# Attention in a stack of layers on one core: a head's 36 key blocks exponentiated in nine chunks of four instead of twelve chunks by tile

## The chip, the cores and the metric

One core of one Trainium2 chip runs the whole program. The metric is the device time of one execution in microseconds. It has five engines with queues of their own: TensorE (PE, matmuls), VectorE (DVE), ScalarE (ACT), GpSimd (POOL) and SyncE (SP, which issues DMAs).

## The reference, cut to what matters

The program computes a stack of layers on 1024 tokens of 512 features: a feed-forward layer, a Mamba2 layer, feed-forward layers again, attention, and a last feed-forward layer. The change touches the attention's heads alone. For each of 32 heads of 16 features (8 key/value heads):

```
draft = einsum(q, k) + causal
_, draft_indices = top_k(draft, 128)
mask = neg except 0 at draft_indices; neg above the diagonal
scores = einsum(q, k) / sqrt(16) + mask
attn = softmax(scores)
out = attn @ v
```

So each row of the 1024 x 1024 causal triangle keeps its 128 largest scores, and the softmax runs over these.

## The kernel before, in words

A head's triangle is cut into 8 tiles of 128 query rows; tile t has t + 1 key blocks of 128, 36 blocks in all. The function `attention_heads_fast` (from line 1824) runs rounds n, and in one round four heads are at different stages. Each engine has its own program, written out by hand; an engine waits on semaphores in the order of its program and nothing overtakes.

- Head n + 1: PE makes its scores into `ps_z` (`scores`, L1933), and DVE copies them to `z` and takes the row maxima (`evacuate`, L2216). Tile 0 is first, with a small `sample` (L1922); these begin the round.
- Heads n, n - 1: ACT counts how many scores lie above a trial cut, four sweeps of seven ACTIVATEs each in a round (`count`, L2052); POOL moves the cuts after each sweep (`move`, L2132) and hands over the final cut (L2171) after the fourth.
- Head n - 2: for tiles 1 to 7 DVE marks what is above the cut (`take`, L2229), PE makes the scores again with the marks (`marked_scores`, L1949) into `ps_m`, DVE finds the eight largest that are left and replaces them (`pick`, L2247: MAX8 at L2256, MATCH_REPLACE8 at L2264), writing `picked`. `marked_scores` of a tile waits for the `pick` before it, and `pick` waits for `marked_scores`. Tile by tile DVE runs `pick(t)`, `evacuate(t)`, `take(t + 2)`.
- Head n - 3: PE makes the exponents transposed into one of two PSUM tiles `ps_e` (`exponents`, L1982), ACT exponentiates them into one of three slots of `eT` (`exponential`, L2067, the ACTIVATE at L2074), and PE multiplies by v (`add_v`, L2007, the matmul at L2016; 32-bit, 17 columns, two matmul instructions a block). After the last chunk DVE divides (`divide`, L2267) in the next round.
- The row maxima of head n - 2 are turned by PE (`turned_rows`, L1970) and copied by ACT to `rows` in two halves (`row_out`, L2077). The second half ends ACT's round, and it waits until the last chunk's exponents of head n - 3 are made.

A head's exponents come in chunks. Before, a chunk is up to four blocks of one tile, so there are 12: of 1, 2, 3, 4 blocks for tiles 0 to 3, and 4 + 1, 4 + 2, 4 + 3, 4 + 4 for tiles 4 to 7. For each chunk PE issues one matmul a block from `picked` (L1995, not for tile 0), one wide matmul with the row maxima (L1997), one a block for the scores (L2000) and one for the diagonal block (L2003). `turn_and_add` (L2020) makes the exponents of a chunk and then `add_v` of the chunk two before. PE's round, from L2028:

```
if live(n - 3): turn_and_add(n - 3, CHUNK_AHEAD)          # chunk 0
if live(n + 1): scores(n + 1, 0); sample(n + 1)
if live(n - 3): turn_and_add(n - 3, CHUNKS_FIRST)         # chunk 1
for t in range(1, NT):
    marked_scores(n - 2, t)
    turn_and_add(n - 3, CHUNKS_AFTER_MARKED[t])
    scores(n + 1, t)
    if t in (2, 7): turned_rows(n - 2, t // 7)
    turn_and_add(n - 3, CHUNKS_AFTER_SCORES[t])
```

On ACT `EXP_BEFORE` (L1845) spreads the exponentials evenly over the 28 counts of a round, by the columns counted; each round does them one chunk late (`LATER`).

Of the kernel before, what the change touches and what calls it, by code (L numbers as in the profile page):

```python
# [15 lines left out]
ACT = mybir.ActivationFunctionType  # L16
AX = mybir.AxisListType

P = 128
S = 1024  # L20
D = 512
NT = S // P
# [24 lines left out]
REP = AH // KVH  # L47
# [1776 lines left out]
def attention_heads_fast(nc, env, X, qT, kT, v, mixed, q_tok, k_sums):  # L1824

    W = NT - 1
    OFF = [P * (t * (t + 1) // 2 - 1) for t in range(NT + 1)]
    FAR = 2.0 ** 20
    BIG = 1024.0
    RING = 3  # L1830
    CHUNKS = [(t, b) for t in range(NT) for b in range(0, t + 1, 4)]
    NCH = len(CHUNKS)
    LAST_CHUNK = [max(i for i, (u, _) in enumerate(CHUNKS) if u == t) for t in range(NT)]
    CHUNK_AHEAD = (0,)
    CHUNKS_FIRST = (1,)
    CHUNKS_AFTER_MARKED = ((), (), (), (), (), (7,), (9,), ())
    CHUNKS_AFTER_SCORES = ((), (2,), (3, 4), (5,), (6,), (8,), (10,), (11,))
    LATER = 1
    SWEEPS = ((0, 0), (1, 2), (0, 1), (1, 3))
    FIRST, LAST = -1, AH + 3  # L1840
# [6 lines left out]
    with ExitStack() as ctx:  # L1847
# [8 lines left out]
        picked = env.picked  # L1856
# [63 lines left out]
        @block.tensor  # L1920
        def _(pe):
            def sample(h):  # L1922

                if h >= 4:
                    pe.wait_ge(rows_done, 2 * (h - 3))
                if h >= 1:
                    pe.wait_ge(stats_done, 3 * h)
                for t in range(1, NT):
                    last = pe.matmul(ps_sample[:, t - 1, :], qT[:, h, t * P:(t + 1) * P], k_sums[:, h // REP, t, :],
                                     start=t == 1, stop=True, skip_group_check=True)  # L1930
                last.then_inc(sampled, 1)

            def scores(h, t):  # L1933

                L, at = (t + 1) * P, z_at(t)
                done = h * NT + t - (0 < t < 4)
                if done:
                    pe.wait_ge(z_done, done)
                for n in range(0, L, BANK):
                    w = min(BANK, L - n)  # L1940
                    diagonal = n + w == L
                    if diagonal:
                        pe.matmul(ps_z[:, at + L - P:at + L], env.ident_bf[:], env.future_bf[:], start=True, stop=False,
                                  skip_group_check=True)
                    last = pe.matmul(ps_z[:, at + n:at + n + w], qT[:, h, t * P:(t + 1) * P], kT[:, h // REP, n:n + w],  # L1945
                                     start=not diagonal, stop=True, skip_group_check=True)
                last.then_inc(s_done, 1)

            def marked_scores(h, t):  # L1949

                L, at = (t + 1) * P, m_at(t)
                pe.wait_ge(take_done, h * W + t)
                done = h * W + t - 1 - (1 < t < 4)
                if done:
                    pe.wait_ge(pick_done, done)
                for n in range(0, L, BANK):
                    w = min(BANK, L - n)
                    diagonal = n + w == L
                    if diagonal:
                        pe.matmul(ps_m[:, at + L - P:at + L], env.ident_bf[:], env.future_bf[:], start=True, stop=False,  # L1960
                                  skip_group_check=True)
                    pe.matmul(ps_m[:, at + n:at + n + w], qT[:, h, t * P:(t + 1) * P], kT[:, h // REP, n:n + w],  # L1962
                              start=not diagonal, stop=False, skip_group_check=True)
                for n in range(0, L, BANK):
                    w = min(BANK, L - n)
                    last = pe.matmul(ps_m[:, at + n:at + n + w], ident_taken[:], mark[:, (h * W + t) % 2, n:n + w], start=False, stop=True,  # L1966
                                     skip_group_check=True)
                last.then_inc(marked, 1)

            def turned_rows(h, half):  # L1970

                pe.wait_ge(split_done, h + 1)
                if half == 0 and h + 3 < AH:
                    pe.wait_ge(stats_done, 3 * (h + 4))
                elif half or h:
                    pe.wait_ge(rows_done, 2 * h + half)
                for t in range(4):
                    last = pe.matmul(ps_x[:, t * P:(t + 1) * P], parts[:, 4 * half + t, :], env.ident_bf[:],
                                     start=t == 0, stop=True, skip_group_check=True)
                last.then_inc(row_done, 1)  # L1980

            def exponents(h, i):  # L1982

                t, b0 = CHUNKS[i]
                w = min(4, t + 1 - b0)
                g = h * NCH + i
                if g >= 2:
                    pe.wait_ge(exp_done, g - 1)
                pe.wait_ge(rows_done, 2 * h + 1 + t // 4)
                out = ps_e[g % 2]  # L1990
                if t:
                    pe.wait_ge(pick_done, h * W + t)
                    for b in range(w):
                        at = OFF[t] + (b0 + b) * P
                        pe.matmul(out[:, b, :], picked[:, h % 2, at:at + P], ident_back[:], start=b == 0, stop=False,  # L1995
                                  skip_group_check=True)
                pe.matmul(out[:, 0:w, :], minus_rows[:], rows[:, t * P:(t + 1) * P].unsqueeze(1).to_broadcast([P, w, P]),  # L1997
                          start=t == 0, stop=False, skip_group_check=True)
                for b in range(w):
                    last = pe.matmul(out[:, b, :], kT[:, h // REP, (b0 + b) * P:(b0 + b + 1) * P], qT[:, h, t * P:(t + 1) * P],  # L2000
                                     start=False, stop=True, skip_group_check=True)
                if b0 + w == t + 1:
                    last = pe.matmul(out[:, w - 1, :], env.future_bf[:], env.ident_bf[:], start=False, stop=True,  # L2003
                                     skip_group_check=True)
                last.then_inc(et_done, 1)

            def add_v(g):  # L2007

                h, i = divmod(g, NCH)
                t, b0 = CHUNKS[i]  # L2010
                w = min(4, t + 1 - b0)
                pe.wait_ge(exp_done, g + 1)
                if i == 0 and h:
                    pe.wait_ge(divided, h)
                for b in range(w):
                    last = pe.matmul(ps_o[:, t, :], eT[:, g % 3, b * P:(b + 1) * P], v[:, b0 + b, h // REP, :],  # L2016
                                     start=i == 0 and b == 0, stop=b0 + b == t, skip_group_check=True)
                last.then_inc(av_done, 1)

            def turn_and_add(h, chunks):  # L2020

                for i in chunks:
                    exponents(h, i)
                    if h * NCH + i >= 2:
                        add_v(h * NCH + i - 2)

            pe.wait_ge(set_up, SET_UP)
            for n in range(FIRST, LAST):  # L2028
                if live(n - 3):
                    turn_and_add(n - 3, CHUNK_AHEAD)  # L2030
                if live(n + 1):
                    scores(n + 1, 0)
                    sample(n + 1)
                if live(n - 3):
                    turn_and_add(n - 3, CHUNKS_FIRST)
                for t in range(1, NT):
                    if live(n - 2):
                        marked_scores(n - 2, t)
                    if live(n - 3):
                        turn_and_add(n - 3, CHUNKS_AFTER_MARKED[t])  # L2040
                    if live(n + 1):
                        scores(n + 1, t)
                    if live(n - 2) and t in (2, 7):
                        turned_rows(n - 2, t // 7)
                    if live(n - 3):
                        turn_and_add(n - 3, CHUNKS_AFTER_SCORES[t])
            add_v(AH * NCH - 2)
            add_v(AH * NCH - 1)

        @block.scalar  # L2050
        def _(act):
# [14 lines left out]

            def exponential(g):  # L2067

                t, b0 = CHUNKS[g % NCH]
                w = min(4, t + 1 - b0)  # L2070
                act.wait_ge(et_done, g + 1)
                if g >= 3:
                    act.wait_ge(av_done, g - 2)
                act.activation(eT[:, g % 3, 0:w * P], ps_e[g % 2][:, 0:w, :].rearrange("p b q -> p (b q)"), ACT.Exp,  # L2074
                               scale=0.25).then_inc(exp_done, 1)

            def row_out(h, half):  # L2077
# [6 lines left out]
            for n in range(FIRST, LAST):  # L2084
                at = 0
# [364 lines left out]
```

## Time and profile before

| | |
|---|---|
| median of 3 runs | 3192.2 us (3191.99 to 3193.25) |
| the profiled execution, its own time | 3191.56 us |
| its span | 3189.8 us |
| mean granted TensorE clock | 0.949 of full |
| busy over the whole span | PE 90%, DVE 73%, ACT 62%, POOL 48% |
| the heads' rounds | from 2058.8 us (first row maximum of tile 0) to about 3064 us |
| ACTIVATEs at L2074, whole run | 384 (12 a head) |
| matmul instructions at L2016, whole run | 2304 (72 a head) |

The span is divided by engine busy time, and a share is an average over the whole program; the heads take the last third. Times in a row are from the span's start.

### The profile page before, as it was taken

What the parts mean: (1) busy time and instruction counts of PE and PEld (TensorE: products, weight loads), DVE (VectorE), ACT (ScalarE), POOL (GpSimd) and SP (SyncE); (2) the same over time, 40 slices, a digit from 0 to 9 for tenths busy, and PEclk for the clock granted to TensorE, in tenths of its full rate; (3) what the DMA queues carried; (4) which work ended last, traced back from release to release, by engine and by line L of the source; (5) the groups of instructions that cost most, each with busy time, mean ns of one, the idle gap of its engine ahead of it and who ended that gap; (6) DMA issues with size and microseconds to landing.
All of it is one profiled execution on the core that took longest, in us unless ns stands there. A gap on an engine that the chain in (4) does not pass through costs nothing. (4 is left out here: it accounts for less than half of the span.)

```text
span 3189.8 us, 50575 instructions
## 1 busy us (share of the span) xinstructions
PE 2886.2 (90%) x15929; PEld 1745.3 (55%) x15929; DVE 2319.5 (73%) x4516; ACT 1984.2 (62%) x4218; POOL 1539.0 (48%) x3659
## 2 busy tenths in 40 slices
PE   8899999999999999999999989748888888888779
PEld 4455455454464554554554544426666666666654
DVE  6666676676776766766766767758888888888746
ACT  2464554564554645545645623589999999999823
POOL 3235234253253352342442544677777777777503
PEclk9999999999999999999999999859988988988889
DMA  2222232132132231322322410000000000000010
GB/s 95 60 83 90 73 104 75 66 119 86 64 109 80 80 99 66 98 81 73 110 63 73 118 37 27 1 1 2 2 2 2 2 2 2 2 2 2 1 51 27
DMA packets 65804, 169.63 MB, mean 53 GB/s; under 512 B 11776, under 2 KB 19328, under 8 KB 64512
## 3 DMA queue, kind: packets, MB, share of 16 engines
q1 hardware_dynamic: 54448, 115.17, 11.3%
q10 hardware_dynamic: 11088, 51.19, 4.6%
q8 instruction: 132, 2.16, 0.3%
q14 instruction: 136, 1.11, 0.1%
HBM read 161.08 MB, written 5.24 MB: 52 GB/s over the span
## 5 line engine op out<-in xcount | busy, mean ns | idle before, releaser
L2063 ACT ACTIVATE X<-ah_z,ah_trial 128x256 bf16<-128x256 f32 (+6 forms) x896 | 732.9, 824 | 23.9 <-POOL ah_trial L2166 14.3
L1212 ACT ACTIVATE m_mix<-m_mix,m_cs 128x128 f32<-128x128 f32 x1024 | 312.5, 388 | 33.0 <-DMA m_mix<-cs_rows 32.7
L2016 PE MATMUL ah_ps_o<-a_v,X 128*128 128x17 f32 x2304 | 318.9, 265 | 0.2 <-DVE hT L2274 0.2
L2016 PEld LDWEIGHTS ah_ps_o<-a_v,X 128*128 128x128 f32 x2304 | 303.4, 200 | 0.3 <-issue 0.3
L1094 POOL TENSOR_TENSOR m_xdec<-m_xdt,m_decay_out 128x512 f32<-128x512 f32 x112 | 118.4, 1057 | 336.2 <-DVE m_xdt L1338 202.4
L1224 ACT ACTIVATE m_squares<-m_gate 128x512 f32<-128x512 f32 x128 | 80.5, 629 | 316.4 <-DVE m_gate L1376 316.2
L2256 DVE MAX8 ah_top<-ah_ps_m 128x8 f32<-128x256 f32 (+6 forms) x224 | 186.2, 831 | 73.2 <-PE ah_ps_m L1966 68.7
L1016 PE MATMUL m_ps_d<-m_w_out,m_gate 128*128 128x512 f32 x512 | 233.5, 599 | 0.0
L1016 PE MATMUL m_ps_x<-m_w_out,m_gate 128*128 128x512 f32 x512 | 233.0, 598 | 0.0
L2074 ACT ACTIVATE X<-ah_ps_e 128x512 f32<-128x512 f32 (+3 forms) x384 | 184.9, 482 | 53.7 <-PE ah_ps_e L2003 44.8
L1122 POOL TENSOR_TENSOR m_squares<-m_squares 128x256 f32<-128x256 f32 x128 | 92.9, 726 | 255.0 <-ACT m_squares L1224 255.0
L2235 DVE TENSOR_SCALAR_CACHE_REDUCE X<-ah_z,ah_cut 128x256 bf16<-128x256 f32 (+6 forms) x224 | 193.5, 874 | 26.2 <-POOL ah_cut L2171 26.2
L1962 PE MATMUL ah_ps_m<-a_kT,a_qT 128*128 128x512 bf16 (+3 forms) x352 | 117.2, 372 | 97.2 <-DVE tables L2264 97.2
L1338 DVE TENSOR_TENSOR m_xdt<-m_ps_y,m_dt 128x512 f32<-128x512 f32 x128 | 87.6, 690 | 160.4 <-PE m_ps_y L957 160.4
L2158 POOL TENSOR_TENSOR ah_slope<-ah_between,ah_table 128x7 f32<-128x7 f32 x128 | 193.3, 1511 | 0.0
L2226 DVE TENSOR_SCALAR_CACHE_REDUCE ah_z<-ah_ps_z 128x256 f32<-128x256 f32 (+6 forms) x224 | 182.5, 816 | 13.9 <-PE ah_ps_z L1945 13.9
L2264 DVE MATCH_REPLACE8 tables<-ah_top,ah_ps_m 128x256 bf16<-128x256 f32 (+6 forms) x224 | 182.5, 815 | 0.3 <-issue 0.3
L1345 DVE TENSOR_TENSOR m_mix<-m_mix,m_cb 128x1024 f32<-128x1024 f32 x128 | 176.8, 1381 | 4.6 <-ACT m_mix L1215 4.4
L2063 ACT ACTIVATION_READ_ACCUMULATOR X<-ah_z,ah_trial 128x1 f32 x896 | 176.9, 197 | 0.0
L1185 ACT ACTIVATE m_xbc<-m_xbc 128x1024 f32<-128x1024 f32 x80 | 84.6, 1057 | 148.4 <-DVE m_xbc L1321 148.2
L1079 POOL TENSOR_TENSOR m_xdt<-m_w_proj 128x256 f32<-128x256 f32 x32 | 23.8, 742 | 287.1 <-PE m_ps_d L885 287.1
L1321 DVE SCALAR_TENSOR_TENSOR m_xbc<-m_b_tok,m_conv_p,m_xbc 128x1023 f32<-128x1023 f32 (+2 forms) x96 | 129.7, 1351 | 44.6 <-ACT m_xbc L1177 42.4
(318 smaller groups left out, 7470.9 us busy)
## 6 DMA issues: line engine op xcount, KB each, us to landing
m_mix<-cs_rows SPq DMA_DIRECT2D x128, 512.0 KB, 4.0
m_w_proj<-in_w_proj ACTq DMA_DIRECT2D x69, 512.0 KB, 3.3
m_fade<-fade_rows SPq DMA_DIRECT2D x224, 128.0 KB, 3.9
m_w_out<-in_w_out ACTq DMA_DIRECT2D x7, 2048.0 KB, 7.8
X<-in_x SPq DMA_DIRECT2D x8, 256.0 KB, 5.9
m_w_out<-in_w_out SPq DMA_DIRECT2D x1, 2048.0 KB, 9.9
x_away<-X SPq DMA_DIRECT2D x1, 2048.0 KB, 7.3
X<-x_away SPq DMA_DIRECT2D x8, 256.0 KB, 6.1
```

The costliest lines, as they stand in the source:

```text
L1016: last = pe.matmul(ps_out[c % 2], gate[:, half * 4 + i, c * P:(c + 1) * P], w_out[:, half * 4 + i, :], start=(half == 0 and i == 0), stop= ...
L1212: act.activation(mix[:, u % 3, h, :], mix[:, u % 3, h, :], ACT.Relu, bias=cs[:, c, h0 + h:h0 + h + 1], scale=-1.0).then_inc(lag_done, 1)
L1321: op = dve.scalar_tensor_tensor(out=acc, in0=src[:, 0:S - n], scalar=conv_p[:, g, j, TAPS - 1 - n:TAPS - n], in1=acc, op0=ALU.mult, op1=AL ...
L1345: dve.tensor_tensor(mix[:, u % 3], mix[:, u % 3], cb[:, c, :].unsqueeze(1).to_broadcast([P, HU, P]), ALU.mult).then_inc(mix_done, 1)
L2016: last = pe.matmul(ps_o[:, t, :], eT[:, g % 3, b * P:(b + 1) * P], v[:, b0 + b, h // REP, :], start=i == 0 and b == 0, stop=b0 + b == t, s ...
L2063: act.activation(sign[:, at % 2, 0:(t + 1) * P], z[:, h % RING, cols(t)], ACT.Sign, bias=trial[:, h % RING, 0, t - 1:t], scale=-1.0, accum ...
L2074: act.activation(eT[:, g % 3, 0:w * P], ps_e[g % 2][:, 0:w, :].rearrange("p b q -> p (b q)"), ACT.Exp, scale=0.25).then_inc(exp_done, 1)
L2158: pool.tensor_tensor(slope[:, 0], between[:, 1], table[:, 5], ALU.pow).then_inc(own, 1)
L2226: dve.tensor_scalar(z[:, h % RING, cols(t)], ps_z[:, z_at(t):z_at(t) + (t + 1) * P], 0.0, NEG, ALU.add, ALU.max, accum_out=row_max[:, h % ...
L2235: dve.tensor_scalar(mark[:, (h * W + t) % 2, 0:(t + 1) * P], z[:, h % RING, cols(t)], cut[:, h % 2, t - 1:t], 0.0, ALU.is_ge, ALU.add, acc ...
L2256: dve.max(top[:, r], ps_m[:, m_at(t):m_at(t) + (t + 1) * P]).then_inc(pick_step, 1)
L2264: dve.match_replace(picked[:, h % 2, cols(t)], top[:, r], ps_m[:, m_at(t):m_at(t) + (t + 1) * P], TAKEN).then_inc(pick_done, 1)
```

## The change

It cuts the 36 blocks, in order of tile and block, into nine chunks of four. A chunk may then hold blocks of up to three tiles: (0,0) (1,0) (1,1) (2,0) | (2,1) (2,2) (3,0) (3,1) | (3,2) (3,3) (4,0) (4,1) | (4,2) (4,3) (4,4) (5,0) | (5,1) to (5,4) | (5,5) (6,0) (6,1) (6,2) | (6,3) to (6,6) | (7,0) to (7,3) | (7,4) to (7,7). For each tile in a chunk the matmul with the row maxima is issued apart, so there are 15 of them a head instead of 12. On PE, chunk 0 and 1 keep their places, and chunks 2 to 8 are issued one after each `scores(t)`, t from 1 to 7. ACT's nine exponentials are spread by the same formula. The first waits of a chunk are for the last tile in it.

```diff
-    CHUNKS = [(t, b) for t in range(NT) for b in range(0, t + 1, 4)]
+    BLOCKS = [(t, b) for t in range(NT) for b in range(t + 1)]
+    CHUNKS = [BLOCKS[i:i + 4] for i in range(0, len(BLOCKS), 4)]
     NCH = len(CHUNKS)
-    LAST_CHUNK = [max(i for i, (u, _) in enumerate(CHUNKS) if u == t) for t in range(NT)]
+    LAST_CHUNK = [max(i for i, blocks in enumerate(CHUNKS) if (t, t) in blocks) for t in range(NT)]
     CHUNK_AHEAD = (0,)
     CHUNKS_FIRST = (1,)
-    CHUNKS_AFTER_MARKED = ((), (), (), (), (), (7,), (9,), ())
-    CHUNKS_AFTER_SCORES = ((), (2,), (3, 4), (5,), (6,), (8,), (10,), (11,))
+    CHUNKS_AFTER_SCORES = ((), (2,), (3,), (4,), (5,), (6,), (7,), (8,))
...
             def exponents(h, i):
-                t, b0 = CHUNKS[i]
-                w = min(4, t + 1 - b0)
                 g = h * NCH + i
                 if g >= 2:
                     pe.wait_ge(exp_done, g - 1)
-                pe.wait_ge(rows_done, 2 * h + 1 + t // 4)
+                pe.wait_ge(rows_done, 2 * h + 1 + CHUNKS[i][-1][0] // 4)
+                pe.wait_ge(pick_done, h * W + CHUNKS[i][-1][0])
                 out = ps_e[g % 2]
...
+                tiles = sorted(dict(CHUNKS[i]))
+                for t in tiles:
+                    places = [n for n, block in enumerate(CHUNKS[i]) if block[0] == t]
+                    lo, w = places[0], len(places)
...
+                    pe.matmul(out[:, lo:lo + w, :], minus_rows[:], rows[:, t * P:(t + 1) * P].unsqueeze(1).to_broadcast([P, w, P]),
+                              start=first, stop=False, skip_group_check=True)
...
             def add_v(g):
...
-                for b in range(w):
-                    last = pe.matmul(ps_o[:, t, :], eT[:, g % 3, b * P:(b + 1) * P], v[:, b0 + b, h // REP, :],
-                                     start=i == 0 and b == 0, stop=b0 + b == t, skip_group_check=True)
+                for n, (t, b) in enumerate(CHUNKS[i]):
+                    last = pe.matmul(ps_o[:, t, :], eT[:, g % 3, n * P:(n + 1) * P], v[:, b, h // REP, :],
+                                     start=i == 0 and n == 0, stop=b == t, skip_group_check=True)
...
-                    if live(n - 3):
-                        turn_and_add(n - 3, CHUNKS_AFTER_MARKED[t])
...
-                act.activation(eT[:, g % 3, 0:w * P], ps_e[g % 2][:, 0:w, :].rearrange("p b q -> p (b q)"), ACT.Exp,
+                act.activation(eT[:, g % 3], ps_e[g % 2][:].rearrange("p b q -> p (b q)"), ACT.Exp,
                                scale=0.25).then_inc(exp_done, 1)
```

## Rows read from the trace of the kernel before

**Rows 1.** Busy time by window: PE, PEld, DVE, ACT, POOL, granted clock, DMA, GB/s:
```profile
2170.50:2941.00 770.50, 640.90 (x5908) 518.48 (x5906) 673.74 (x1795) 741.22 (x1822) 571.21 (x2055) 0.90 0.01 2
...
2377.80:2406.50 28.70, 23.74 (x234) 19.27 (x231) 25.95 (x70) 28.08 (x70) 22.02 (x80) 0.94 0.01 2
2406.50:2436.70 30.20, 24.91 (x233) 20.15 (x230) 25.93 (x70) 28.83 (x73) 21.96 (x80) 0.89 0.01 2
2436.70:2466.50 29.80, 24.85 (x230) 20.07 (x227) 25.82 (x69) 28.39 (x71) 21.88 (x80) 0.89 0.01 2
...
2438.00:2444.80 6.80, 5.78 (x38) 4.57 (x37) 6.18 (x24) 6.14 (x17) 5.95 (x25) 0.50 0.02 4
```
**Rows 2.** Line L2222, one instruction a round: count, first and last start:
```profile
L2222 DVE TENSOR_REDUCE ah_row_max<-ah_ps_z x27: 291/291/292, 2170.5 to 2941.0; 128x1 f32<-128x128 f32 x27
```
**Rows 3.** Waits, 2170.5 to 2941.0: who waited for whom, us, times, longest:
```profile
PE ah_ps_m L1962 <- DVE tables L2264: 75.2, 102, 1.2
DVE ah_top L2256 <- PE ah_ps_m L1966: 53.3, 78, 2.1
...
ACT X L2074 <- PE ah_ps_e L2003: 18.8, 41, 1.0
DVE ah_inv L2272 <- PE ah_ps_o L2016: 17.8, 26, 1.2
...
ACT ah_rows L2082 <- PE ah_ps_e L2003: 9.9, 26, 0.6
```
**Rows 4.** Timeline of ACT: start, us, engine, line, operation, shapes:
```profile
2434.70 0.58 ACT L2074 ACTIVATE X<-ah_ps_e 128x512 f32<-128x512 f32 x1
2435.18 0.61 ACT L2063 ACTIVATE X<-ah_z,ah_trial 128x384 bf16<-128x384 f32 x1
...
2437.30 0.26 ACT L2074 ACTIVATE X<-ah_ps_e 128x128 f32<-128x128 f32 x1
2437.45 0.93 ACT L2063 ACTIVATE X<-ah_z,ah_trial 128x768 bf16<-128x768 f32 x1
```
**Rows 5.** Timeline of DVE in a long round:
```profile
2438.08 0.21 DVE L2272 RECIPROCAL ah_inv<-ah_ps_o 128x8 f32<-128x8 f32 x1 [0.57 <-PE ah_ps_o L2016]
...
2438.53 0.47 DVE L2235 TENSOR_SCALAR_CACHE_REDUCE X<-ah_z,ah_cut 128x256 bf16<-128x256 f32 x1
...
2447.03 0.70 DVE L2256 MAX8 ah_top<-ah_ps_m 128x8 f32<-128x512 f32 x1 [1.90 <-PE ah_ps_m L1966]
```
**Rows 6.** Timeline of POOL at the same place:
```profile
2438.19 0.21 POOL L2171 TENSOR_TENSOR ah_cut<-ah_trial,ah_slope 128x7 f32<-128x7 f32 x1
```
**Rows 7.** Timeline of PE in that long round:
```profile
2436.33 0.23 PE L1943 MATMUL ah_ps_z<-future_bf,ident_bf 128*128 128x128 bf16 x1 [1.05 <-DVE ah_z L2226]
...
2436.64 0.27 PE L1995 MATMUL ah_ps_e<-ah_ident_back,tables 128*128 128x128 bf16 x2
...
2437.02 1.02 PE L2016 MATMUL ah_ps_o<-a_v,X 128*128 128x17 f32 x8
2439.06 0.29 PE L1960 MATMUL ah_ps_m<-future_bf,ident_bf 128*128 128x128 bf16 x1 [1.02 <-DVE X L2235]
...
2440.96 0.55 PE L2016 MATMUL ah_ps_o<-a_v,X 128*128 128x17 f32 x2
2441.35 0.27 PE L1960 MATMUL ah_ps_m<-future_bf,ident_bf 128*128 128x128 bf16 x1
...
2446.28 0.22 PE L1960 MATMUL ah_ps_m<-future_bf,ident_bf 128*128 128x128 bf16 x1
```
**Rows 8.** Timeline of PE in a short round, chunk 4 and its add_v:
```profile
2384.88 0.38 PE L1995 MATMUL ah_ps_e<-ah_ident_back,tables 128*128 128x128 bf16 x4
...
2385.54 0.79 PE L2016 MATMUL ah_ps_o<-a_v,X 128*128 128x17 f32 x6
2386.18 0.22 PE L1960 MATMUL ah_ps_m<-future_bf,ident_bf 128*128 128x128 bf16 x1
```
**Rows 9.** Timeline of DVE in that short round:
```profile
2386.94 0.70 DVE L2256 MAX8 ah_top<-ah_ps_m 128x8 f32<-128x512 f32 x1 [0.64 <-PE ah_ps_m L1966]
```

More of the change, by code:

```diff
@@ L1988, in exponents @@
                     pe.wait_ge(exp_done, g - 1)
-                pe.wait_ge(rows_done, 2 * h + 1 + t // 4)
+                pe.wait_ge(rows_done, 2 * h + 1 + CHUNKS[i][-1][0] // 4)
+                pe.wait_ge(pick_done, h * W + CHUNKS[i][-1][0])
                 out = ps_e[g % 2]
-                if t:
-                    pe.wait_ge(pick_done, h * W + t)
-                    for b in range(w):
-                        at = OFF[t] + (b0 + b) * P
-                        pe.matmul(out[:, b, :], picked[:, h % 2, at:at + P], ident_back[:], start=b == 0, stop=False,
-                                  skip_group_check=True)
@@ L1997, in exponents @@
-                pe.matmul(out[:, 0:w, :], minus_rows[:], rows[:, t * P:(t + 1) * P].unsqueeze(1).to_broadcast([P, w, P]),
-                          start=t == 0, stop=False, skip_group_check=True)
-                for b in range(w):
[L2000 to L2004, printed above, removed]
+                tiles = sorted(dict(CHUNKS[i]))
@@ new lines, in exponents @@
+                first = True
+                for t in tiles:
+                    places = [n for n, block in enumerate(CHUNKS[i]) if block[0] == t]
+                    lo, w = places[0], len(places)
+                    b0 = CHUNKS[i][lo][1]
+                    if t:
+                        for b in range(w):
+                            at = OFF[t] + (b0 + b) * P
+                            pe.matmul(out[:, lo + b, :], picked[:, h % 2, at:at + P], ident_back[:], start=first, stop=False,
+                                      skip_group_check=True)
+                            first = False
+                    pe.matmul(out[:, lo:lo + w, :], minus_rows[:], rows[:, t * P:(t + 1) * P].unsqueeze(1).to_broadcast([P, w, P]),
+                              start=first, stop=False, skip_group_check=True)
+                    first = False
+                    for b in range(w):
+                        last = pe.matmul(out[:, lo + b, :], kT[:, h // REP, (b0 + b) * P:(b0 + b + 1) * P],
+                                         qT[:, h, t * P:(t + 1) * P], start=False, stop=True, skip_group_check=True)
+                    if b0 + w == t + 1:
+                        last = pe.matmul(out[:, lo + w - 1, :], env.future_bf[:], env.ident_bf[:], start=False, stop=True,
+                                         skip_group_check=True)
@@ L2009, in add_v @@
                 h, i = divmod(g, NCH)
-                t, b0 = CHUNKS[i]
-                w = min(4, t + 1 - b0)
                 pe.wait_ge(exp_done, g + 1)
@@ L2014, in add_v @@
                     pe.wait_ge(divided, h)
-                for b in range(w):
-                    last = pe.matmul(ps_o[:, t, :], eT[:, g % 3, b * P:(b + 1) * P], v[:, b0 + b, h // REP, :],
-                                     start=i == 0 and b == 0, stop=b0 + b == t, skip_group_check=True)
+                for n, (t, b) in enumerate(CHUNKS[i]):
+                    last = pe.matmul(ps_o[:, t, :], eT[:, g % 3, n * P:(n + 1) * P], v[:, b, h // REP, :],
+                                     start=i == 0 and n == 0, stop=b == t, skip_group_check=True)
                 last.then_inc(av_done, 1)
@@ L2067, in exponential @@
             def exponential(g):
-                t, b0 = CHUNKS[g % NCH]
-                w = min(4, t + 1 - b0)
                 act.wait_ge(et_done, g + 1)
```

## The prediction

> **What bounds the kernel now.** The busy shares of the whole span put PE first, but they mix layers with different limits. What counts is the window view of 26 rounds of heads [rows 1, 2]: 770.5 us / 26 = 29.63 us a round, with ACT busy for 741.2 us of it (96%), DVE for 673.7 (87%), PE for 640.9 (83%). So ACT looks like the bound, with 741.22 / 26 = 28.51 us of work a round, and the change takes instructions from ACT. The Trainium skill (Perfetto Trace Analysis, Identifying the Most-Contended Engine) says to optimize the engine of highest occupancy first; by that, ACT is the place.
>
> The waits say otherwise [rows 3]. ACT's listed waits are all for PE: 18.8 us before an exponential, 9.9 before the row copy that ends its round, 1.1 us a round together. I find no listed wait of DVE or PE for ACT or POOL in these rounds. They wait for each other: PE 75.2 us for DVE's replaced maxima, DVE 53.3 us for PE's marked scores and 17.8 us for PE's last add_v before the division. Two engines that wait only for each other set their own length, and ACT follows with 1.1 us to spare. DVE is the longer half, 673.7 / 26 = 25.9 us of work a round, and its waits for PE are what can be won or lost.
>
> Where do these lie? In a long round 1.90 us is before the MAX8 of tile 3, and 0.57 before the division [rows 5]; in a short round the first is 0.64 [rows 9]. The windows show why [rows 1]. The long rounds (30.2 and 29.8 us, mean 30.0) have a mean granted clock of 0.89, the short one (28.7) 0.94. The low level, 1.2 of 2.4 GHz, lasts 6.8 us in a long round (the window at 0.50) and 2 x 0.06 x 28.7 = 3.4 us in the short one. Such a low spell follows two idle times of PE of 1.05 and 1.02 us [rows 7], and it covers the stretch in which PE has most to do before DVE can go on. With x the share of short rounds, 28.7 x + 30.0 (1 - x) = 29.63 makes x 0.28.
>
> **The change, part by part**, at full clock unless said.
>
> *ACT.* From start to next start an exponential of four blocks takes 0.48 us and one of one block 0.15 [rows 4]: 0.11 a block and 0.04 an instruction. Three instructions fewer save 3 x 0.04 = 0.12 us a round (ends: 0, and 3 x 0.15 = 0.45), some 4 us in 32 heads. ACT isn't on the path, so I count 0. Its idle time before exponentials should also go, since PE now makes chunks ahead of their places; what ACT wins it gives back at the row copy, which still waits for PE's last chunk.
>
> *PE's ring.* Exponents of chunk i wait for the exponential of chunk i - 2. By the kernel's formula exponential i starts (i + 1.3) x 28.4 / 9 us into ACT's round, which began at about 2434.2, 0.5 us before its first exponential [rows 4]: exponential 2 at 2444.6, over at 2445.2. PE reaches chunk 4 about 0.66 us after 2446.28 [rows 7], and perhaps 1.2 us earlier without a stall there, 2445.7. Tight, but later tiles have 75.2 / 102 = 0.7 us of idle time before each marked scores [rows 3], which covers a miss: 0, at worst 0.3 a round. The new wait of chunk 2 is for the second half of the row copy, over at 2434.2, and chunk 2 comes after 2439.06 [rows 7], 5 us later: 0. No DMA is issued or moved, and the queues of SP and POOL aren't touched.
>
> *The opening.* A chunk of four blocks of one tile takes 0.66 us and 3 blocks of add_v take 0.64, so 0.21 a block [rows 8]. Chunk 0 grows from one block to four of three tiles (+0.55, the two further row matmuls and diagonals in it), and the add_v before it from three blocks to four (+0.21). These 0.76 us stand in front of scores(0), where PE idles 1.05 us [rows 7]: 0, with 0.29 us of cover left. Chunk 1 grows from two blocks (0.38 us, 2436.64 to 2437.02, [rows 7]) to four with a diagonal (0.66 + 0.05): +0.33 us ahead of the add_v for which the division waits. DVE waits there already, and its next work is the first take of the round. POOL's cut is written from 2438.19 to 2438.40 and the take starts at 2438.53 [rows 5, 6], so nothing else held it. All of the 0.33 is on the path; at the low clock 0.67.
>
> *From the first to the third marked scores* PE works without a pause, 2439.06 to 2446.28 = 7.22 us [rows 7]. Chunk 2 gets one block more (+0.17), its add_v goes from 1 block to 4 (+0.64), that of chunk 1 from 2 to 4 (+0.43); old chunk 4 (0.66) and an add_v of 3 blocks (0.64) leave the stretch: -0.06 us. At the low clock a chunk's matmuls take double, and a block of add_v 0.39 (2440.96 to 2441.35, [rows 7]): 0.33 + 5 x 0.39 - 1.32 - 1.17 = -0.2. I take -0.1 (ends: -0.6, and +0.4 where the cover on DVE's side runs out at tile 2 first).
>
> *The later tiles.* After scores(3) PE has three blocks of a chunk more (+0.5), and 0.7 us of idle time for them; after tiles 5 and 6 it has less than before. 0; without that cover +0.5.
>
> *The clock.* Two things pull apart here, and no row shows which wins. PE's first idle time shrinks from 1.05 to 0.3 us, which speaks for fewer low spells. But the second stays at 1.02 or more, and the low stretch now carries eight blocks of 17-column add_v (four after chunk 2, four after chunk 3) where three stood (1 + 2). In the short round the clock rose again when PE had run chunk 2 with a single such block; that form doesn't come any more. The Trainium skill (TensorE: Matmul & The Clock Gate, What's actually happening) has the low level as the default, which activity lifts; no price follows from that here. I expect the spell in every round and the short form gone: 30.0 - 29.63 = +0.37 a round. In half the rounds I let it last another 3.4 us. Such an addition cost 30.0 - 28.7 = 1.3 us where nothing covered it; here it falls on tiles 3 and 4, with idle time beside it, and I take 0.8, so 0.4 a round. Ends: -1.2 (no spells, ACT binds) and +2.
>
> *Sum.* 0.33 - 0.1 + 0.37 + 0.4 = +1.0 us a round. 28 rounds have all four stages (n from 3 to 30), the three after them a part of it: I count 29, so +29 us. The profiled execution took 3191.56 us (its span 3189.8), 0.6 below the median: **3221 us**, 0.9% slower.
>
> **The rivals.**
>
> *The clock holds, and ACT binds: faster.* Place: the start of a round, between scores(0) and the first marked scores. If the filled idle time keeps the clock at its upper level, DVE's stalls at tiles 2 and 3 vanish. DVE's round is then 28.7 - 0.64 + 0.33 = 28.4 us and ACT's 28.51 - 0.12 = 28.4; both give -1.2 us a round, 29 x 1.2 = 35, so 3156 us. It decides from the point at which most rounds lose their low spell. For it: the idle times of 0.7 us before later marked scores are not followed by low spells in these rounds. Against: the 1 us before the first marked scores doesn't shrink. The occupancy rule above leads to the same place by another way, work taken from ACT. Chance 0.25.
>
> *The spells stay as they are.* 0.33 - 0.1 = +0.23 a round, 3198 us. For it: the two effects on the clock cancel. Chance 0.16.
>
> *The low clock feeds itself.* If PE at the low level, with four blocks of add_v to each chunk, becomes the longer half through tiles 3 to 5 too, the last term is 2 instead of 0.4: +2.6 a round, 3267 us. Against: it needs PE's later idle time gone in all rounds. Chance 0.12.
>
> The forecast has 0.47.
>
> **How the numbers follow.** About 0.2% (6.4 us) is what a measurement of this kernel can tell from no change. Faster by more than that: the first rival, 0.25. Within it: most of the second rival and a little of the forecast's low side, 0.13. Slower: the rest, 0.62. The forecast's own range is 3200 to 3240. To hold 8 in 10 the range goes some way toward both outer rivals: 3165 to 3250 leaves out over half of the first and most of the last.
>
> **What would show it.** Right: ACT's idle time before L2074 nearly gone, and that before L2082 at 1.5 us a round or more; the wait before L2272 up by 0.3; the MAX8 of 384 columns waiting over 1 us; a granted clock of 0.88 or lower over the rounds, and rounds of 30.6 us. Wrong: a granted clock of 0.95 or more with rounds near 28.4, and DVE waiting for POOL's cut; or matmuls of L1995 that wait for the exponentials at L2074, which would make the ring the new bound.

## The result, and the profile after

The changed kernel takes 3250.84 us (median of 4 runs, 3248.0 to 3254.28) against 3192.09 before: a ratio of 1.0182, 95% interval 1.0169 to 1.0194. The forecast was 3221. The profiled execution has a span of 3246.2 us, 56.4 more than before.

The windows of the changed kernel, with the columns of [rows 1]; first 26 rounds, then one ordinary round, then two neighbouring rounds, then low spells:

```profile
2170.40:2993.20 822.80, 688.43 (x5907) 568.06 (x5982) 673.13 (x1795) 737.29 (x1747) 576.89 (x2060) 0.85 0.01 2
2672.20:2702.90 30.70, 25.39 (x233) 20.95 (x234) 25.84 (x69) 28.30 (x68) 22.12 (x79) 0.89 0.01 2
2358.60:2392.00 33.40, 28.34 (x232) 23.68 (x232) 25.83 (x69) 29.78 (x72) 22.70 (x82) 0.79 0.01 1
2392.00:2428.10 36.10, 32.22 (x234) 26.48 (x234) 26.06 (x69) 26.76 (x64) 22.12 (x79) 0.67 0.00 1
2675.00:2681.80 6.80, 6.80 (x45) 5.80 (x45) 4.70 (x20) 6.80 (x17) 6.05 (x22) 0.50 0.02 5
2384.90:2412.20 27.30, 26.05 (x164) 22.37 (x163) 15.97 (x49) 20.20 (x48) 16.75 (x59) 0.50 0.01 2
```

The same 26 rounds as in [rows 1, 2] take 822.8 us instead of 770.5: 31.65 us a round instead of 29.63, at a granted clock of 0.85 instead of 0.90. DVE's work is unchanged (673.1 against 673.7), ACT's is 3.9 us less (737.3 against 741.2: the three instructions a round), and both engines only wait more. By the starts of the rounds and the granted clock in the trace, twelve of the 26 rounds are like the second row, 30.7 us (one 31.1) with one low spell of 6.8 us (called ordinary below), and five take 29.1 us with a spell of 3.4 us. But one spell, in the last row, lasts 27.3 us across two rounds, and in it PE is busy nearly all the time and DVE 16.0 of 27.3 us. In the 26 rounds there are three such spells, and a shorter one of 17 us in the first.

Where DVE waits is in its groups by shape, the same 26 rounds (busy, mean ns, idle before it and who ended it):

```profile
L2256 DVE MAX8 ah_top<-ah_ps_m 128x8 f32<-128x640 f32 x26 | 21.5, 828 | 5.2 <-PE ah_ps_m L1966 5.2
L2256 DVE MAX8 ah_top<-ah_ps_m 128x8 f32<-128x512 f32 x26 | 18.2, 700 | 25.3 <-PE ah_ps_m L1966 25.3
L2256 DVE MAX8 ah_top<-ah_ps_m 128x8 f32<-128x384 f32 x26 | 14.7, 566 | 40.9 <-PE ah_ps_m L1966 40.9
...
L2222 DVE TENSOR_REDUCE ah_row_max<-ah_ps_z 128x1 f32<-128x128 f32 x27 | 7.9, 292 | 26.3 <-PE ah_ps_z L1945 26.3
L2272 DVE RECIPROCAL ah_inv<-ah_ps_o 128x8 f32<-128x8 f32 x26 | 5.4, 208 | 27.7 <-PE ah_ps_o L2020 27.7
```

For comparison the same view of the kernel before:

```profile
L2256 DVE MAX8 ah_top<-ah_ps_m 128x8 f32<-128x640 f32 x26 | 21.5, 829 | 0.0
L2256 DVE MAX8 ah_top<-ah_ps_m 128x8 f32<-128x512 f32 x26 | 18.2, 700 | 35.2 <-PE ah_ps_m L1966 35.2
L2256 DVE MAX8 ah_top<-ah_ps_m 128x8 f32<-128x384 f32 x26 | 14.7, 567 | 7.8 <-PE ah_ps_m L1966 7.7
...
L2222 DVE TENSOR_REDUCE ah_row_max<-ah_ps_z 128x1 f32<-128x128 f32 x27 | 7.9, 291 | 10.3 <-PE ah_ps_z L1945 10.3
L2272 DVE RECIPROCAL ah_inv<-ah_ps_o 128x8 f32<-128x8 f32 x26 | 5.4, 208 | 17.8 <-PE ah_ps_o L2016 17.8
```

The five rows grow by 5.2 - 9.9 + 33.1 + 16.0 + 9.9 = 54.3 us, against 52.3 us for the stretch. So the loss is time in which DVE waits for PE. The 16.0 us before the first row maximum come only from rounds that begin in or just after a late low spell (1.5 to 3.4 us each); in the others that wait is 0.38 us, as before. The largest row is the MAX8 of 384 columns, tile 2: behind the first marked scores PE now has chunk 2 and four blocks of add_v. The timeline of PE in the ordinary round:

```profile
2674.94 0.27 PE L1960 MATMUL ah_ps_m<-future_bf,ident_bf 128*128 128x128 bf16 x1 [1.02 <-DVE X L2235]
...
2675.75 0.42 PE L1999 MATMUL ah_ps_e<-ah_ident_back,tables 128*128 128x128 bf16 x2
...
2677.14 1.84 PE L2020 MATMUL ah_ps_o<-a_v,X 128*128 128x17 f32 x8
2678.81 0.27 PE L1960 MATMUL ah_ps_m<-future_bf,ident_bf 128*128 128x128 bf16 x1
...
2682.66 0.22 PE L1960 MATMUL ah_ps_m<-future_bf,ident_bf 128*128 128x128 bf16 x1
```

At the low clock the chunk takes 1.39 us (2675.75 to 2677.14) and its add_v 1.67 (to 2678.81), where one block took 0.39 [rows 7]. DVE waits 1.91 us for what follows. ACT, in turn, idles 63.2 us before the row copy (9.9 in [rows 3]), 2.4 us a round:

```profile
ACT ah_rows L2082 <- PE ah_ps_e L2009: 63.2, 26, 3.7
...
ACT X L2074 <- PE ah_ps_e L2006: 21.1, 22, 2.1
```

### The profile page after: what moved, and what is told of

Read it like the earlier page. It is cut to its first block and busy times, and to the rows that moved or that the text cites. A ratio compares the mean times of both kernels' runs of the same rounds, so it can differ in the third digit from the quotient of the medians.

```text
span 3246.2 us, 50374 instructions
## 1 busy us (share of the span) xinstructions
PE 2938.0 (91%) x15919; PEld 1801.0 (55%) x16025; DVE 2317.8 (71%) x4516; ACT 1978.7 (61%) x4122; POOL 1542.6 (48%) x3659
## 5 line engine op out<-in xcount | busy, mean ns | idle before, releaser
L2020 PE MATMUL ah_ps_o<-a_v,X 128*128 128x17 f32 x2304 | 330.6, 277 | 0.0
L2020 PEld LDWEIGHTS ah_ps_o<-a_v,X 128*128 128x128 f32 x2304 | 320.6, 215 | 0.1
L2256 DVE MAX8 ah_top<-ah_ps_m 128x8 f32<-128x256 f32 (+6 forms) x224 | 186.0, 830 | 100.9 <-PE ah_ps_m L1966 97.6
L2074 ACT ACTIVATE X<-ah_ps_e 128x512 f32<-128x512 f32 x288 | 169.9, 590 | 57.1 <-PE ah_ps_e L2006 51.1
L1962 PE MATMUL ah_ps_m<-a_kT,a_qT 128*128 128x512 bf16 (+3 forms) x290 | 96.8, 369 | 117.3 <-DVE tables L2264 117.3
L2006 PE MATMUL ah_ps_e<-a_qT,a_kT 128*128 128x128 bf16 x1152 | 163.4, 243 | 0.0
L2002 PE MATMUL ah_ps_e<-ah_rows,ah_minus_rows 128*128 128x256 bf16 (+3 forms) x480 | 162.9, 339 | 0.0
```

The source lines that it names most:

```text
L2006: last = pe.matmul(out[:, lo + b, :], kT[:, h // REP, (b0 + b) * P:(b0 + b + 1) * P], qT[:, h, t * P:(t + 1) * P], start=False, stop=True, ...
L2020: last = pe.matmul(ps_o[:, t, :], eT[:, g % 3, n * P:(n + 1) * P], v[:, b, h // REP, :], start=i == 0 and n == 0, stop=b == t, skip_group_ ...
L2074: act.activation(eT[:, g % 3], ps_e[g % 2][:].rearrange("p b q -> p (b q)"), ACT.Exp, scale=0.25).then_inc(exp_done, 1)
L2256: dve.max(top[:, r], ps_m[:, m_at(t):m_at(t) + (t + 1) * P]).then_inc(pick_step, 1)
```

## The experiments

Theory 1 is that of the forecast: DVE and PE hold each other up, and what counts is what stands on PE before a result for DVE, priced by the clock. Rival 1: the ring of exponents and exponentials, or ACT's work, binds. Rival 2: the new chunks cost by themselves, with their extra row matmuls, wherever they stand. Medians of before beside them are 3192.0 to 3193.0 us.

**Is it ACT?** e7_more_act, the changed kernel:

```diff
+                if g % NCH in (0, 1):
+                    act.wait_ge(spare_done, 2 * (g // NCH) + g % NCH)
+                    act.activation(exp_spare[:], ps_e[g % 2][:].rearrange("p b q -> p (b q)"), ACT.Exp,
+                                   scale=0.25).then_inc(spare_done, 1)
```

> The changed kernel with the exponentials of chunks 0 and 1 done twice (the first into a spare tile): 2 x 0.48 = 0.96 us more of ACT a round. Theory 1: ACT has 2.4 us of idle time before the row copy, so it takes the place of idle time and the time stays at 3251 (+-8, the pattern of the clock). If ACT's work counts (rival 1, and the reading that took work from ACT to be worth something): +0.96 x 29 = +28, 3279 us.

3254.4 us (3240.61 to 3255.76), ratio 1.0195 (1.0177 to 1.0214). The added work is there, the time is not:

```profile
2172.80:2985.40 812.60, 676.18 (x5905) 558.51 (x5980) 672.39 (x1794) 757.36 (x1795) 574.05 (x2056) 0.87 0.01 2
```

ACT is busy 20.1 us longer in 26 rounds than in the changed kernel and the rounds are no longer. (This is the shortest of the four executions, with two of the 27.3 us spells; its ordinary rounds take 30.7 us, as in the changed kernel.) ACT's idle time before the row copy shrinks from 63.2 to 45.6 us instead. Added work of ACT costs nothing here, which fits that taking some away gained nothing. Rival 1 falls as far as ACT's work goes.

**What stands where.** e1_add_first lets the add_v for which the division waits go before the exponents of chunk 1; e2_chunks_later moves the chunks:

```diff
                 for i in chunks:
+                    if i == 1 and h:
+                        add_v(h * NCH + i - 2)
                     exponents(h, i)
-                    if h * NCH + i >= 2:
+                    if h * NCH + i >= 2 and i != 1:
```

> The changed kernel with add_v of the last chunk put before the exponents of chunk 1 instead of behind them. Theory 1 (DVE and PE hold each other up, and what stands on PE in front of a result for DVE counts): the wait before the division falls from about 0.9 us to 0.2 us a round, so -0.6 x 29 = -17 us, about 3233 us; the clock's pattern may move, +-10. Rival 1 (the ring of exponents and exponentials binds): no change, 3251. Rival 2 (the new chunks cost wherever they stand, by their extra row matmuls): no change, 3251.

3228.4 us (3221.38 to 3234.66), ratio 1.0114 (1.0094 to 1.0133): 22 us less than the changed kernel, where 17 was expected. That is not the opening's doing alone, because the pattern of the clock changed with it: in the 26 rounds there are now ten low spells of 17.1 us, eight of them beginning some 3 us into a round, while twelve rounds begin no spell at all. The division's wait falls from 27.7 to 8.4 us in 26 rounds:

```profile
L2274 DVE RECIPROCAL ah_inv<-ah_ps_o 128x8 f32<-128x8 f32 x26 | 5.4, 208 | 8.4 <-PE ah_ps_o L2020 8.4
```

```diff
-    CHUNKS_AFTER_SCORES = ((), (2,), (3,), (4,), (5,), (6,), (7,), (8,))
+    CHUNKS_AFTER_SCORES = ((), (), (2,), (3,), (4,), (5,), (6, 7), (8,))
```

> The changed kernel with chunks 2 to 8 one tile later: none after scores(1), chunks 6 and 7 both after scores(6), where PE idles 1.6 us now. Theory 1: the chunk and the four blocks of add_v leave the stretch before the second and third marked scores (2.75 us at the low clock), the wait of 1.9 us before the MAX8 of 384 columns goes, rounds come to about 28.9 us, 29 x -2 and the long low stretches gone: 3175 to 3195 us. Rival 1 (ring): exponentials come later on PE's side and closer to ACT's places, ACT waits more: 3255 or more. Rival 2: 3251.

3180.57 us (3176.5 to 3182.27), ratio 0.9961 (0.9947 to 0.9975): the same nine chunks, 70 us faster than the change and faster than before. DVE's waits before all its MAX8 fall from 80.3 to 19.2 us in 26 rounds. Rival 2 falls with this, and rival 1's ring too as the cause of the loss. The ratio of e2 is as low although its granted clock over the rounds is only 0.90, that of before:

```profile
2168.80:2924.30 755.50, 641.70 (x5984) 522.53 (x5981) 673.65 (x1794) 735.40 (x1745) 573.67 (x2058) 0.90 0.01 2
```

The place of the chunks and the clock changed together here; e14 below holds the clock alone.

**How much is add_v?** e6_fewer_add_v does two of four blocks of chunk 0 and one of chunk 1:

```diff
-                for n, (t, b) in enumerate(CHUNKS[i]):
+                for n, (t, b) in enumerate(CHUNKS[i][:{0: 2, 1: 1}.get(i, 4)]):
```

> The changed kernel with five of the eight add_v blocks of chunks 0 and 1 left out (two and one are done), so that the low stretch holds three blocks as before; the output leaves these products out. Theory 1, add_v blocks are what lengthens the low stretch: the wait before the MAX8 of 384 columns falls from 1.9 to about 0.7 us, the low spells of 17 and 27 us go, rounds 29.8 to 30.2 us: 3190 to 3210 us. If the low spells come from where the chunks' exponents stand and not from add_v: 3235 to 3251 us. Rivals 1 and 2: 3251.

3183.3 us (3175.79 to 3190.77), ratio 0.9972 (0.9962 to 0.9982): lower than expected. Five blocks cost 5 x 0.21 = 1.05 us at full clock and about 2 at the low one; 67 us / 29 = 2.3 us a round came back. The wait before the MAX8 of 384 columns is 12.6 us instead of 40.9, that of 512 columns 1.7 instead of 25.3:

```profile
L2256 DVE MAX8 ah_top<-ah_ps_m 128x8 f32<-128x512 f32 x26 | 18.1, 696 | 1.7 <-PE ah_ps_m L1966 1.7
L2256 DVE MAX8 ah_top<-ah_ps_m 128x8 f32<-128x384 f32 x26 | 14.7, 564 | 12.6 <-PE ah_ps_m L1966 12.6
```

No spell in these rounds is longer than 6.8 us, but for one of 17.1 us that begins at the end of the last. So the added add_v blocks are much of the work in the way, and without them the long spells nearly vanish. PE now has 14.7 us of waits for the exponentials (13 times, up to 1.2 us), so the ring is felt once the rest gets shorter.

**The clock itself.** The next versions add matmuls whose result nobody reads, where PE would be idle. The helper and its place behind chunk 1 (e3_fill in the changed kernel, e8_before_fill_one in the one before), and the second place before scores(0) (with the first, in the kernel before: e4_before_fill and its repetition e10_before_fill_again):

```diff
+            def fill(h, times):
+                pe.wait_ge(pick_done, h * W)
+                for _ in range(times):
+                    pe.matmul(ps_m[:, 0:BANK], qT[:, 0, 0:P], kT[:, 0, 0:BANK], start=True, stop=True,
+                              skip_group_check=True)
...
                     turn_and_add(n - 3, CHUNKS_FIRST)
+                    if live(n - 2):
+                        fill(n - 2, 4)
```

```diff
+                if live(n - 3) and live(n + 1):
+                    fill(n - 2, 4)
                 if live(n + 1):
                     scores(n + 1, 0)
```

> The changed kernel with four idle matmuls of 512 columns (into the tile of marked scores, never read) behind the add_v after chunk 1, where PE idles 1.0 us. Nothing is left out. Theory 1 with the low clock as the price: the granted clock over the rounds rises from 0.87 to above 0.97, waits before MAX8 of 384 and 512 columns fall below 0.3 us, rounds of 28.5 to 28.9 us: 3170 to 3190 us. Theory 1 without the clock (PE's work alone): +0 to +10 us. Rivals 1 and 2: no change or a little slower, 3251 to 3260.

3179.53 us (3173.41 to 3184.18), ratio 0.9958 (0.9942 to 0.9975): 71 us less than the changed kernel, with more matmuls and no work removed. The granted clock rises to 0.95, not above 0.97 as expected:

```profile
2170.60:2930.30 759.70, 637.78 (x6089) 510.78 (x6086) 669.41 (x1794) 732.01 (x1745) 573.86 (x2060) 0.95 0.01 2
```

The early spells are gone; those left begin 23 to 24 us into a round, four of them of 13.7 us.

> The kernel before, with four idle matmuls in each of its two idle times of 1 us (before scores(0) and behind the add_v after chunk 1). Theory 1 with the clock: its low spells vanish, waits at tiles 2 and 3 go (61 of them, 43 us in 26 rounds), ACT becomes the bound at about 28.5 us a round: 3192 - 29 x 1.1 = 3160 us. Without the clock as a cause: 3192 to 3200 us.

3158.33 us (3158.01 to 3158.37, and one far off), ratio 0.9892 (0.9872 to 0.9912), against 3160 expected. The rounds take 738.5 / 26 = 28.40 us, the clock is at 0.99, ACT is busy 735.5 of 738.5 us, and DVE now waits for POOL's cut, 26 times:

```profile
2169.80:2908.30 738.50, 632.02 (x6117) 490.53 (x6114) 669.69 (x1795) 735.49 (x1823) 572.14 (x2056) 0.99 0.01 2
```

```profile
DVE X L2246 <- POOL ah_cut L2182: 22.9, 26, 1.3
```

With the clock held, ACT is the bound at last. One of its four executions took 8003.5 us; the repetition was made to see whether that comes again.

> The kernel before with idle matmuls in both places once more, unchanged, for its interval and for whether an execution far from the others comes again. Expected 3158 us, +-1.

3159.52 us (3159.25 to 3160.03), ratio 0.9899 (0.9881 to 0.9917). It didn't come again in four executions; its cause stays open.

> The kernel before with four idle matmuls only behind the add_v after chunk 1; the idle time before scores(0) stays. Theory 1: the clock falls in fewer rounds than before but in more than with both filled; between 3160 and 3185 us. If one of the two idle times alone is enough to bring the spell, either about 3190 (this one does nothing) or 3158 (this one does all).

3191.48 us (3190.17 to 3193.89), ratio 0.9998 (0.9989 to 1.0008): this place alone does nothing. The clock stays at 0.90; the spells only begin earlier in the round, by 0.7 us or more. So in the kernel before the place behind chunk 1 is not enough; whether the one before scores(0) would do alone was not tried.

**What starts the long spells?** They begin 26.3 to 26.7 us into a round of the changed kernel, after the two largest idle times of PE, before the marked scores of tiles 6 and 7. Here they are in the round whose low spell starts at 2384.9:

```profile
2379.03 0.38 PE L1962 MATMUL ah_ps_m<-a_kT,a_qT 128*128 128x512 bf16 x1 [1.20 <-DVE tables L2264]
2383.58 0.38 PE L1962 MATMUL ah_ps_m<-a_kT,a_qT 128*128 128x512 bf16 x1 [1.63 <-DVE tables L2264]
```

Before they were about 0.7 us. Between the marked scores of tiles 5 and 6 PE now has exponents and add_v of four blocks each, where it had six and five; between those of 6 and 7 four each, where it had seven and six. These idle times are in every ordinary round too, mostly without a spell behind them, so they are not the whole condition. Ahead of two of the three long spells one of them was longer than usual (1.46 instead of 1.20, 1.92 instead of 1.63). e13_late_fill:

```diff
                         turn_and_add(n - 3, CHUNKS_AFTER_SCORES[t])
+                        if t in (5, 6) and live(n - 2):
+                            late_fill(4 if t == 5 else 6)
```

> The changed kernel with idle matmuls (376 columns each, into unused columns of the bank of ps_o) where it has its late idle times: four behind the chunk after scores(5), six behind the one after scores(6). The low spell of each round stays. If the spells that begin at 26.7 us into a round and last up to 27 us are started by these late idle times (1.2 and 1.6 us): none of them comes, all rounds are 30.7 us or shorter, 3250.8 - 4 x 8 = 3219 us, +-8. If they are started by something else: 3245 to 3255 us.

3225.53 us (3223.15 to 3226.35), ratio 1.01 (1.0083 to 1.0117). After a spell of 17 us in the first of the rounds none is longer than 6.8, and the 26 rounds take 802.5 / 26 = 30.87 us with the clock at 0.88:

```profile
2169.70:2972.20 802.50, 699.32 (x6171) 562.77 (x6245) 673.68 (x1794) 736.21 (x1747) 576.04 (x2065) 0.88 0.01 2
```

Without the late idle times none of the 27 us spells comes, and they cost 25 us of the 59. e14_fill_both has this and the four matmuls behind chunk 1:

> The changed kernel, its chunks where they are, with idle matmuls in all its long idle times: behind the add_v after chunk 1 and at the two late places. Theory 1: the clock is the whole loss apart from PE's blocks at full clock; no low spells in nearly all rounds, ACT binds with 28.3 us a round: 3155 to 3165 us, level with the kernel before with idle matmuls. If the places of the new chunks cost at full clock too: 3170 or more.

3153.22 us (3149.02 to 3154.78), ratio 0.9877 (0.9861 to 0.9894), 97.6 us below the changed kernel and a little below what was expected, with every chunk in its place. So with the clock held at its upper level the places of the new chunks cost nothing, and the loss goes through the clock. It is the fastest version of the study:

```profile
2168.30:2903.00 734.70, 638.22 (x6248) 504.75 (x6349) 669.74 (x1794) 731.48 (x1745) 574.73 (x2058) 0.99 0.01 2
```

734.7 / 26 = 28.26 us a round, ACT busy 99.6% of it. Against the old chunks with the clock held (28.40) that is 0.14 us less, and 4.0 / 26 = 0.15 us of it is ACT's own work (731.5 against 735.5): there the change gives what it takes from ACT.

**Four versions that missed.** e11_before_even moves chunk 4 of the kernel before behind the third marked scores:

```diff
-    CHUNKS_AFTER_MARKED = ((), (), (), (), (), (7,), (9,), ())
-    CHUNKS_AFTER_SCORES = ((), (2,), (3, 4), (5,), (6,), (8,), (10,), (11,))
+    CHUNKS_AFTER_MARKED = ((), (), (), (4,), (), (7,), (9,), ())
+    CHUNKS_AFTER_SCORES = ((), (2,), (3,), (5,), (6,), (8,), (10,), (11,))
```

> The kernel before with chunk 4 issued after the third marked scores instead of before them; its twelve chunks stay. Theory 1: what stands on PE between the first and third marked scores is what counts. 0.66 us of chunk 4 and 0.64 of add_v leave it (double at the low clock), the 35 us of waits before the MAX8 of 512 columns in 26 rounds mostly go: -1.0 to -1.3 us a round, 3155 to 3170 us. Rivals 1 and 2 have nothing to say here; if the stretch doesn't count, 3192.

3185.86 us (3183.72 to 3186.99), ratio 0.9978 (0.9968 to 0.9988): a fifth to a third of what was expected. The rounds are 0.34 us shorter, but the clock is lower than before, 0.87 instead of 0.90. In 26 rounds the waits before MAX8 fall from 53.3 to 24.5 us, and the one before the division grows from 17.8 to 31.3, because many spells now begin at the end of a round and reach over the opening:

```profile
2172.20:2933.70 761.50, 648.99 (x5908) 527.46 (x5905) 675.47 (x1794) 739.89 (x1822) 573.23 (x2057) 0.87 0.01 2
```

e5_all combines e1, e2, and both fills; e9_later_and_fill is e5 without the one before scores(0); e12_short_opening also moves chunk 1 behind scores(1).

> The changed kernel with add_v first at chunk 1, chunks one tile later, and four idle matmuls in each of the two places. Theory 1: no low spells in most rounds, DVE waits only for POOL's cut, ACT binds with its own work: 28.26 us a round as in the kernel before with idle matmuls, less 0.12: 3150 to 3157 us. Rival 1 (ring binds): ACT waits for PE's chunks once they come later, 3165 or more. Rival 2 (row matmuls, wherever they stand): no better than the kernel before with idle matmuls, 3160 or more.

3168.35 us, ratio 0.9931 (0.9912 to 0.995).

> As the version with everything (3168 us), but without the idle matmuls before scores(0), where PE has only 0.25 us of idle time with the new chunks. Theory 1: the wait before the first row maximum falls back from 0.85 to 0.4 us, ACT binds in most rounds at 28.3 us or a little less: 3155 to 3165 us. If the later chunks are what costs there: 3168 or more.

3169.33 us, ratio 0.9929 (0.9911 to 0.9946): the fill before scores(0) made no difference.

> The changed kernel with chunk 1's exponents after scores(1), the add_v of the last chunk alone at its old place with four idle matmuls behind it, chunks 2 to 5 one tile later, 6 and 7 after scores(6). Theory 1: the division waits under 0.3 us, no chunk but one before the second marked scores, ACT binds: 3150 to 3160 us. If the ring binds, since chunk 1 comes only just before its place on ACT: ACT waits before L2074, 3165 or more.

3184.8 us (3180.93 to 3195.98), ratio 0.998 (0.9969 to 0.9992). Over their 26 rounds the granted clock is 0.95 in e5 and e9 and 0.90 in e12, against 0.99 in e14, which moves no chunk. (The profiled execution of e12 took 3192.93 us, 8 more than its median.) In e5 and e9 the low spells mostly begin some 11 us into a round.

All three came out where their expectations put the case that the later chunks, or the ring, cost time, and the waits bear this out in part. Once DVE waits for POOL's cut, as it does here, ACT is on the path, and then its waits for late exponents count:

```profile
ACT X L2085 <- PE ah_ps_e L2006: 5.0, 10, 0.8
ACT X L2085 <- PE ah_ps_e L2009: 4.5, 12, 0.5
```

```profile
DVE X L2246 <- POOL ah_cut L2182: 34.2, 25, 1.9
ACT X L2085 <- PE ah_ps_e L2006: 22.3, 25, 1.0
ACT X L2085 <- PE ah_ps_e L2009: 4.7, 9, 0.7
```

The first two rows are the waits of ACT before exponentials in e9, 9.5 us in 26 rounds of together 745.5 us; the other three are from e12, whose 26 rounds take 765.1. In e14 no such wait of ACT is listed, and its rounds take 734.7 us. So in e9 those waits are most of the 10.8 us between the two, and in e12 they are 27.0 of 30.4 us. How much of them is the later place of the chunks and how much the low clock wasn't separated. Rival 2 has nothing from this, as e14 has the same matmuls.

## Why the prediction was right and wrong

*What binds.* Right. DVE and PE wait for each other, ACT's work isn't on the path: shown by e7, and by the row copy's idle time (2.4 us a round; forecast 1.5 or more). ACT's waits before its exponentials were forecast as nearly gone and are 21.1 us against 18.8; 22 waits now, of up to 2.1 us.

*ACT, 0.12 us a round, counted 0.* Right in both: 737.3 against 741.2 us of work is 0.15 a round, and it showed only in e14, where ACT binds.

*PE's ring, 0.* Right for the changed kernel: in these rounds no matmul has a listed wait for the exponentials. In e1 and e6 there are some (7.4 and 14.7 us).

*The opening, +0.33.* Right: the division waits 27.7 instead of 17.8 us, +0.38 a round. Ahead of scores(0) PE's idle time is 0.26 us in the ordinary round, where 0.29 was forecast. The 22 us of e1 can't be set against this term, since the clock's pattern moved as well.

*From the first to the third marked scores, -0.1.* Wrong in size. The stretch took 7.22 us [rows 7] and takes 2682.66 - 2674.94 = 7.72 us in the ordinary round, +0.5. Two things were missed. The low spell begins at about 2675.0, with the stretch (in [rows 1, 7] at 2438.0, 1.1 us ahead of it), so 1.1 us more of it falls on this work; and four blocks of add_v take 1.67 us there, not 4 x 0.39. DVE pays it at tile 2 first, which was named as the upper end of this term: the MAX8 of 384 columns waits 1.91 us in that round.

*An ordinary round.* Forecast 29.63 + 1.0 = 30.6 us, measured 30.7, the sum of one term too small and one too large, so the agreement is luck. Had all 26 been so, they would have taken 798 us, 28 more than before.

*The later tiles, 0, and the clock, +0.37 and +0.4.* This is the step that failed. It let the spell "last another 3.4 us" in half the rounds and took 0.8 us for that, as if it always began in the opening. What happened is that ordinary rounds kept spells of 6.8 us, and that from time to time one began at the end of a round, where the text had counted the later tiles as "0" because PE has less to do there. It has less to do, and the idle time that this opens, 1.2 and 1.6 us, is what the spell needs, as e13 shows. Once low there, PE goes into the opening and the add_v blocks at the low clock, and three times stays low for 27 us. Over the 26 rounds all that departs from the ordinary round adds 822.8 - 798 = 25 us, and what lies outside them adds 4 (56.4 - 52.3). Filling the late idle times took 25 us off the whole time. The rival in which the low clock feeds itself named that mechanism and gave 3267 us with a chance of 0.12, but put it into every round. It asked for PE's later idle time to be gone in all rounds; it was gone only inside the long spells, and had grown elsewhere.

The trace of before held a sign of this. The forecast says that the later idle times of 0.7 us are not followed by low spells, and that is so for those. But in one round of the 26 such an idle time is 1.25 us, and a spell of 6.8 us begins 1.0 us after its end, in a round of 30.7 us where the others take 28.6 to 30.2:

```profile
2570.10 0.38 PE L1962 MATMUL ah_ps_m<-a_kT,a_qT 128*128 128x512 bf16 x1 [1.25 <-DVE tables L2264]
...
2571.00:2577.90 6.90, 6.90 (x41) 5.18 (x39) 5.75 (x12) 5.65 (x15) 3.90 (x15) 0.51 0.01 2
```

*The clock holds: 3156 us.* It didn't happen by itself, but the number was good: 3153 in e14 once the idle times behind chunk 1 and at the two late places were filled.

## What to carry to other kernels

Where two engines wait for each other and a third looks busiest, work taken from the third may buy nothing; double some of it as a test. When work is moved out of a stretch of TensorE, count also the idle time it leaves, since the clock that falls there is paid for by the next stretch, and matmuls that nobody reads can be worth more than the work they add (here -71 and -98 us). Before packing work into fewer and fuller pieces, see which result is queued behind each piece.

## What was not expected of the hardware

The pattern of the granted clock goes with the order of work, and small shifts change it as a whole: one filled idle time of two changed nothing (3191.5 us), both gave -34 us. The changed kernel's ordinary rounds are nearly all alike to 0.1 us (30.7), with a spell at the same place each time, until one slips. And TensorE at the low level was busy for 26.05 of 27.3 us without the clock rising, while a stretch of e3 kept the upper level with less. The two shares can't be compared directly, since a block of add_v takes 0.39 us at the low level and 0.21 at the upper; but the busy share alone doesn't tell the level. What of PE's activity decides was not tried. The row of e3's rounds at the upper level:

```profile
2645.00:2667.90 22.90, 18.13 (x178) 14.40 (x175) 21.37 (x62) 22.90 (x57) 18.97 (x65) 1.00 0.01 1
```

There PE is busy 79% of 22.9 us and the clock stays at 1.00.
